# A field-pair interaction tower on one core: sums of eight units, half-height transposes, and a batch cut into five uneven pieces

## What is computed

```python
p = e[:, ROW_IDX]            # first field of each of the 496 pairs
q = e[:, COL_IDX]            # second field
z = jnp.einsum('bne,hne,bnh->bn', p, kernel, q)
h = jnp.concatenate([z, dense_ctx], axis=1)      # 496 + 16 = 512
h = jnp.maximum(h @ W_top1 + b_top1, 0.0)        # 512
h = jnp.maximum(h @ W_top2 + b_top2, 0.0)        # 256
y = h @ W_top3                                   # 1
```

## Time and profile before

| what | us |
|---|---|
| median of 3 runs | 491.37 |
| lowest and highest | 490.74, 492.25 |
| the profiled execution, its own time | 490.84 |
| span of that execution, first to last instruction | 488.7 |
| PE busy | 433.7 |
| DVE busy | 308.0 |
| POOL busy | 242.4 |
| ACT busy | 35.9 |

### The profile page before, as it was taken

How to read it: one execution, slowest core, us unless ns; L and a number is a source line. 1 busy time by engine, 2 the same in 40 slices (tenths; PEclk the granted TensorE clock), 3 DMA queues, 4 the chain that set the end, 5 groups by cost and what they waited for, 6 DMA issues and landing times.

```text
span 488.7 us, 7990 instructions
## 1 busy us (share of the span) xinstructions
PE 433.7 (89%) x3424; PEld 273.8 (56%) x3424; DVE 308.0 (63%) x321; ACT 35.9 (7%) x69; POOL 242.4 (50%) x260
## 2 busy tenths in 40 slices
PE   0227359999999999999999999999999999999986
PEld 0115226665665666666655666666556666666645
DVE  0113418878876646778876547888875557888840
ACT  1000000000001110000001010000001100000002
POOL 5777777777777776651537775462356000000000
PEclk9999859999999999999999999999999999999999
DMA  6677941111111111000101111100001000000000
GB/s 145 155 168 161 213 143 28 29 25 28 28 28 27 26 28 26 24 19 4 24 12 29 26 28 23 20 21 10 15 18 29 0 2 2 2 0 1 1 1 0
DMA packets 13619, 19.18 MB, mean 39 GB/s; under 512 B 5584, under 2 KB 6928, under 8 KB 13584
## 3 DMA queue, kind: packets, MB, share of 16 engines
q1 hardware_dynamic: 5392, 10.27, 8.8%
q0 software_dynamic: 8192, 8.40, 8.2%
HBM read 18.65 MB, written 0.00 MB: 38 GB/s over the span
## 4 chain that ended last, share of the span: by engine, by line
PE 85%; POOL 6%; DMA 3%; issue 2%; SPq 2%; ACT 1%; DVEq 0%; DVE 0%
PE bil L356 47%; PE z_ps L375 24%; POOL gathered L240 6%; PE side_ps L389 4%; PE side_ps L326 4%; PE side_ps L395 2%; DMA inner<-in_dense_rows 2%; PE bil L389 1%; DMA gathered<-in_tbl,ids_sb 1%; SPq L193 1%; PE bil L395 1%; PE side_ps L401 1%; ACT emb L252 0%; DMA ids_sb<-in_ids 0%; DVEq L127 0%
## 5 line engine op out<-in xcount | busy, mean ns | idle before, releaser
L311 DVE TENSOR_TENSOR prod<-bil,emb 128x1024 f32<-128x1024 f32 x224 | 261.4, 1218 | 121.7 <-PE bil L356 121.7
L240 POOL DMA_INDIRECT gathered<-in_tbl,ids_sb x256 | 242.2, 946 | 134.6 <-issue 74.4
L356 PE MATMUL bil<-emb,k_sb 64*128 64x256 f32 x2048 | 250.2, 390 | 3.6 <-ACT emb L252 3.6
L356 PEld LDWEIGHTS bil<-emb,k_sb 64*128 64x128 f32 x2048 | 193.0, 189 | 73.5 <-DVE prod L311 30.7
L375 PE MATMUL z_ps<-prod,sel_sb 128*32 128x512 f32 x960 | 125.9, 604 | 1.6 <-DVE prod L311 1.6
L375 PEld LDWEIGHTS z_ps<-prod,sel_sb 128*32 128x32 f32 x960 | 26.9, 110 | 61.9 <-issue 42.0
L326 PE MATMUL side_ps<-ident_sb,gathered 128*128 128x128 f32 x128 | 22.3, 300 | 31.3 <-DMA gathered<-in_tbl,ids_sb 31.3
L303 DVE TENSOR_TENSOR prod<-bil,emb 128x512 f32<-128x512 f32 x32 | 21.9, 684 | 38.6 <-PE bil L356 29.1
L252 ACT ACTIVATE emb<-side_ps 128x512 f32<-128x512 f32 x32 | 19.2, 599 | 316.6 <-PE side_ps L326 316.6
L375 PE MATMUL z_ps<-inner,sel_sb 128*32 128x512 f32 x64 | 30.2, 619 | 13.7 <-DMA inner<-in_dense_rows 13.7
L326 PEld LDWEIGHTS side_ps<-ident_sb,gathered 128*128 128x128 f32 x128 | 14.3, 148 | 50.0 <-issue 34.0
(11 more groups left out here) (17 smaller groups left out, 22.7 us busy)
## 6 DMA issues: line engine op xcount, KB each, us to landing
k_sb<-in_k_blocks SPq DMA_DIRECT2D x24, 256.0 KB, 5.0
gathered<-in_tbl,ids_sb POOLq DMA_INDIRECT x256, 2.4
k_sb<-in_k_blocks SPq DMA_DIRECT2D x8, 192.0 KB, 5.9
inner<-in_dense_rows SPq DMA_DIRECT2D x64, 1.0 KB
w_sb<-in_w SPq DMA_DIRECT2D x1, 1024.0 KB, 9.2
k_sb<-in_k_blocks SPq DMA_DIRECT2D x8, 64.0 KB, 4.9
w_sb<-in_w SPq DMA_DIRECT2D x1, 512.0 KB, 10.2
ids_sb<-in_ids SPq DMA_DIRECT2D x1, 128.0 KB, 2.1
```

The source lines that it names most:

```text
L240: pool.indirect_dma_start(gathered[:, n % GATHER_RING, t, f * EMBED:(f + 1) * EMBED], None, tables[field], bass.IndirectOffsetOnAxis(ap=id ...
L311: dve.tensor_tensor(out, x_y[:, :, :], both.to_broadcast([P, 2, W]), ALU.mult)\
L356: last = pe.matmul(out[:, s, i * CHUNK:(i + 1) * CHUNK], k_sb[rows, n, :], e[rows, j, :], start=True, stop=True)
```

## The change

Three things change together.

The batch goes through in five pieces, of 128, 128, 256, 256 and 256 samples (`WIDTHS`). All loops over pieces run five times, and in the first two pieces every matmul, product, copy and gather of a quad is half as wide (a quad has four gathers there).

A sum takes eight units instead of four. For that `prod` has twelve places instead of ten and `inner` four instead of two; SP therefore places the dense rows of the first four quads early.

A quad is transposed by pieces of 64 rows: for each tile of 128 samples and each couple, one transpose for the upper 64 samples and one for the lower, with a 64 x 64 part of the identity, into the two banks of a `bil` place. Transposes and units take turns in the ring of three places (`USES`), and each waits for the use three before it: for DVE if that was a unit, for ACT's copy if that was a quad. The copy to `emb` reads both banks of the place and puts the halves in order. `side_ps` is left to the head, whose steps come one unit earlier and no longer wait for the copies of quads.

```diff
-CHUNK = 256
-CHUNKS = BATCH // CHUNK
-SUBS = CHUNK // P
+WIDTHS = [128, 128, 256, 256, 256]
+CHUNKS = len(WIDTHS)
+FROM = [sum(WIDTHS[:q]) for q in range(CHUNKS)]
+CHUNK = max(WIDTHS)
...
-W = 2 * CHUNK
+BANK = 512
...
-BIL_RING, PROD_RING, IN_RING, GATHER_RING = 3, 10, 2, 6
-BATCH_UNITS = 4
+BIL_RING, PROD_RING, IN_RING, GATHER_RING = 3, 12, 4, 6
+BATCH_UNITS = 8
 BATCHES = NUNIT // BATCH_UNITS
-GROUP_BATCHES = 8
+GROUP_BATCHES = 32 // BATCH_UNITS
...
-PIECE_UNITS = [6, 10, 14, 18]
+PIECE_UNITS = [5, 9, 13, 17]
...
+USES = []
+for _u in range(NUNIT):
+    USES += [("quad", n) for n in TRANSPOSED_AT[_u]] + [("unit", _u)]
+BANKS_OF = {use: at % BIL_RING for at, use in enumerate(USES)}
+BEFORE = {use: USES[at - BIL_RING] for at, use in enumerate(USES) if at >= BIL_RING}
...
-        inner = sb("inner", [P, IN_RING, W])
+        inner = sb("inner", [P, IN_RING, 2, CHUNK])
...
-                    for t in range(SUBS):
+                    for t in range(WIDTHS[q] // P):
                         field = 4 * k + f
                         pool.indirect_dma_start(
...
-                act.activation(emb[:, q % 2, 2 * k:2 * k + 2, :].rearrange("p c b -> p (c b)"), side_ps[:, :],
-                               ACT.Copy).then_inc(emb_kept, 1)
+                w = WIDTHS[q]
+                banks = bil[BANKS_OF["quad", n]][:, :, 0:w].rearrange("p s (x b) -> p x s b", b=EMBED)
...
+                act.activation(out, banks, ACT.Copy).then_inc(emb_kept, 1)
...
+                elif w == CHUNK:
+                    both = e[:, c:c + 2, :].rearrange("p c b -> p (c b)").unsqueeze(1)
+                    dve.tensor_tensor(out, x_y[:, :, :], both.to_broadcast([P, 2, BANK]), ALU.mult)\
+                       .then_inc(unit_multiplied, 1)
                 else:
...
+                    both = e[:, c:c + 2, :].unsqueeze(1)
+                    dve.tensor_tensor(out.rearrange("p j (c b) -> p j c b", c=2),
+                                      x_y[:, :, 0:2 * w].rearrange("p j (c b) -> p j c b", c=2),
+                                      both.to_broadcast([P, 2, 2, w]), ALU.mult).then_inc(unit_multiplied, 1)
...
-                if n:
-                    pe.wait_ge(emb_kept, n)
-                pieces = kept_before(u)
-                if pieces:
-                    pe.wait_ge(head_kept, pieces)
+            def wait_banks(use):
+                kind, at = BEFORE.get(use, (None, 0))
+                if kind == "unit":
+                    pe.wait_ge(unit_multiplied, at + 1)
+                elif kind == "quad":
+                    pe.wait_ge(emb_kept, at + 1)
+
+            def transpose_quad(n):
+                pe.wait_ge(quad_gathered[n % GATHER_RING], gathered_count(n))
+                wait_banks(("quad", n))
+                tiles = WIDTHS[n // QUADS] // P
                 for c in range(2):
-                    for t in range(SUBS):
-                        last = pe.transpose(side_ps[:, c * CHUNK + t * P:c * CHUNK + (t + 1) * P],
-                                            gathered[:, n % GATHER_RING, t, c * P:(c + 1) * P], ident_sb[:, :])
+                    for t in range(tiles):
+                        for s in range(2):
+                            rows = slice(s * EMBED, (s + 1) * EMBED)
+                            at = (c * tiles + t) * EMBED
+                            last = pe.transpose(bil[BANKS_OF["quad", n]][:, s, at:at + EMBED],
+                                                gathered[rows, n % GATHER_RING, t, c * P:(c + 1) * P],
+                                                ident_sb[rows, rows])
                 last.then_inc(quad_transposed, 1)
...
-                if u >= BIL_RING:
-                    pe.wait_ge(unit_multiplied, u - BIL_RING + 1)
-                out, e = bil[u % BIL_RING], emb[:, q % 2, :, :]
+                wait_banks(("unit", u))
+                w = WIDTHS[q]
+                out, e = bil[BANKS_OF["unit", u]], emb[:, q % 2, :, 0:w]
...
-                quads = sum(len(TRANSPOSED_AT[v]) for v in range(u + 1))
-                pe.wait_ge(emb_kept, quads)
```

More of the change, by code:

```diff
@@ L153, in interaction_tower @@
         y_sb = sb("y_sb", [P, TILES])
-        bil = [pb(f"bil{i}", [P, 2, W]) for i in range(BIL_RING)]
-        z_ps = pb("z_ps", [P, W])
-        side_ps = pb("side_ps", [P, W])
+        bil = [pb(f"bil{i}", [P, 2, BANK]) for i in range(BIL_RING)]
+        z_ps = pb("z_ps", [P, BANK])
+        side_ps = pb("side_ps", [P, BANK])
         ids_loaded = sem("ids_loaded")
@@ L176, in interaction_tower, with gathered_count @@
         block = ctx.enter_context(nc.Block())
+        def gathered_count(n):
+            return 16 * 4 * sum(WIDTHS[i // QUADS] // P for i in range(n % GATHER_RING, n + 1, GATHER_RING))
         def batch_of(unit):
@@ L290, in _ @@
         def _(dve):
-            dve.memset(inner[:, :, CHUNK:W], 0.0).then_inc(inner_cleared, 1)
+            dve.memset(inner[:, :, 1, :], 0.0).then_inc(inner_cleared, 1)
             for u in range(NUNIT):
                 q, (k, m, c) = u // NU, UNITS[u % NU]
-                x_y, out, e = bil[u % BIL_RING], prod[:, u % PROD_RING, :, :], emb[:, q % 2, :, :]
+                w = WIDTHS[q]
+                x_y, e = bil[BANKS_OF["unit", u]], emb[:, q % 2, :, 0:w]
+                out = prod[:, u % PROD_RING, :, 0:2 * w]
                 dve.wait_ge(unit_done, u + 1)
@@ L302, in _ @@
                         dve.wait_ge(batch_reduced, batch_of(inner_unit(n - IN_RING)) + 1)
[L303 to L305 removed]
+                    dve.tensor_tensor(out[:, 0, :].rearrange("p (j b) -> p j b", j=2), x_y[:, :, 0:w],
+                                      e[:, a:a + 1, :].to_broadcast([P, 2, w]), ALU.mult)
@@ L355, in bilinear @@
                             j = 2 * k + 1 if s == 0 else 2 * k
-                        last = pe.matmul(out[:, s, i * CHUNK:(i + 1) * CHUNK], k_sb[rows, n, :], e[rows, j, :],
+                        last = pe.matmul(out[:, s, i * w:(i + 1) * w], k_sb[rows, n, :], e[rows, j, :],
                                          start=True, stop=True)
@@ L369, in reduce_batch @@
                         col, r = row // 32, row % 32
-                        moving = prod[:, u % PROD_RING, i, :]
+                        moving = prod[:, u % PROD_RING, i, 0:2 * WIDTHS[q]]
                         if m is None and i == 1:
@@ L388, in head @@
                         for g in range(GROUPS):
-                            last = pe.matmul(bank[:, j * CHUNK:(j + 1) * CHUNK], w1_sb[:, g, n * P:(n + 1) * P],
-                                             z_rows(g), start=g == 0, stop=g == GROUPS - 1)
+                            last = pe.matmul(bank[:, j * w:(j + 1) * w], w1_sb[:, g, n * P:(n + 1) * P],
+                                             z_rows(q, g), start=g == 0, stop=g == GROUPS - 1)
                 elif PIECES[i] == "l2":
@@ L394, in head @@
                         for g in range(MT1):
-                            last = pe.matmul(bank[:, n * CHUNK:(n + 1) * CHUNK], w2_sb[:, g, n * P:(n + 1) * P],
-                                             h1_sb[:, g, :], start=g == 0, stop=g == MT1 - 1)
+                            last = pe.matmul(bank[:, n * w:(n + 1) * w], w2_sb[:, g, n * P:(n + 1) * P],
+                                             h1_sb[:, g, 0:w], start=g == 0, stop=g == MT1 - 1)
                 else:
                     pe.wait_ge(head_kept, done + MT1 + MT2)
-                    for t in range(SUBS):
+                    for t in range(w // P):
                         for g in range(MT2):
@@ L417, in _ @@
                 for n in TRANSPOSED_AT[u]:
-                    transpose_quad(u, n)
+                    transpose_quad(n)
                 bilinear(u)
```

47 lines of the change are left out of this document (26 added, 21 removed).

## The result

The changed kernel takes 495.13 us (median; 491.31 for the kernel before beside it), a ratio of 1.0081 with a 95% interval of 1.0066 to 1.0096: slower by 0.8%, as forecast (493, slower). The profiled execution took 493.93 us for a span of 492.1.

What follows compares the result with a forecast made beforehand. It took PE to bound the kernel from 75 us on, after waits for dense features. Start 54.5, then 33.7, 61.3, 101.8, 108.9 and 130.2 gave a 490.4 us span, 493 for the median; range 485.5 to 503.5.

Steps and rivals of the forecast that it cites:

- dense row lands: Start: quad 4's dense row, issued behind k_sb and the head weights, lands at 54.5 us (52.5 to 58).
- piece 1: Second 128-row piece: eight narrow eight-unit batches of 6.54, head 7.1, quads and first copy 1.9; 61.3 us.
- last piece and tail: End of the span: 126.7 before, +5.3 for batches, -3.5 for transposes, +1.7 for a longer last sum; 130.2 us.
- wide batch without a quad: 256-row pieces: eight units and their sum take 11.68 us instead of 11.02, held by DVE through three banks; +0.66.
- narrow batch: 128-row pieces: eight units and their sum take 6.54 us, at a product pitch of 0.62; half of before is 5.51.
- Rival A: Start gains more: dense row near 50.5, before 51.5; median 489 us, or 485 if transposes hide entirely; chance 0.25.
- Rival D: Eight-unit batches are not held by DVE: 10.67 us each, 456 us in all; chance 0.02.
- +5.3 for the batches: 256-row piece: the cost of eight-unit batches, each 0.66 us dearer through DVE's pace.
- -3.5 for the transposes: 256-row piece: 64-row transposes save 0.35 to 0.54 us per quad, 3.5 a piece, with ends of 0 and 4.3.
- the turn in the ring: Transposes sharing the three bil banks wait for DVE, with PE's next units queued behind: up to 0.2 us per quad.
- rival C: Products at 128 rows take 0.69 us apiece, or transposes still cost 0.59: 497 to 503 us; chance 0.20.
- Rival B: Weights bind at 128 columns: a unit stays at 0.86 us, +28, 521 us in all; chance 0.07.

Runs made afterwards that it cites:

- e7: Changed kernel with products of wide units, other than a quad's first, cut to 512 of 1024 elements: 471.58 us in one execution.
- e8: Kernel before with the same cut of wide products to half, as a control: 489.46 us in one execution.
- e1: Changed kernel with sums of four units instead of eight, all else kept: 483.07 us, 0.9835 of the kernel before.
- e6: Kernel before with sums of eight units alone, plus the changed kernel's rings (twelve product places, four dense-row places): 485.25 us, ratio 0.9887.
- e5: Changed kernel with sums of four units, eight places in inner and four wide pieces: 469.20 us, 0.9566 of the kernel before.
- e10: Kernel before with 64-row transposes alone, in the ring of bil, and head steps a unit earlier: 485.50 us, ratio 0.9891.
- e2: Changed kernel with four pieces of 256 rows instead of five uneven ones: 488.25 us, 0.9964 of the kernel before.

## Why the prediction was right, step by step

| step of the sum | predicted, us | measured, us |
|---|---|---|
| dense row lands | 54.5 | 54.30 |
| rest of piece 0 | 33.7 | 34.14 |
| piece 1 | 61.3 | 61.17 |
| piece 2 | 101.8 | 102.17 |
| piece 3 | 108.9 | 109.23 |
| last piece and tail | 130.2 | 131.09 |
| wide batch without a quad | 11.68 | 11.69 |
| narrow batch | 6.54 | 6.41 |
| span | 490.4 | 492.1 |

**The start.** One stall took the place of the other as predicted: the dense row of quad 4 is issued behind all of `k_sb` and the head's weights. Rival A, a landing before 51.5, didn't come about. The SP queue of after shows why (start, duration, line and transfer):

```profile
5.96 29.91 SPq L205 DMA_DIRECT2D k_sb<-in_k_blocks  x38
...
37.10 6.93 SPq L233 DMA_DIRECT2D w_sb<-in_w  x1
44.07 1.29 SPq L234 DMA_DIRECT2D b_sb<-in_b  x1
45.41 1.23 SPq L235 DMA_DIRECT2D b_sb<-in_b  x1
46.68 11.73 SPq L217 DMA_DIRECT2D inner<-in_dense_rows  x10
```

`k_sb` is issued by 35.9 and the two large head weights by 37.1; three tiny transfers then hold SP until 46.68, and the row lands 7.6 us after that. But issued is not landed. For the weight transfers the DMA view of after gives size and us from issue to landing (the one of 512 KB took 17.0), and the windows show the DMA engines until then:

```profile
w_sb<-in_w SPq DMA_DIRECT2D x1, 1024.0 KB, 17.2
...
w_sb<-in_w SPq DMA_DIRECT2D x1, 1.0 KB, 16.8
```

```profile
12.00:48.00 36.00, 24.68 (x296) 20.05 (x294) 17.94 (x36) 2.30 (x6) 27.31 (x29) 1.00 1.05 230
48.00:53.00 5.00, 0.00 (x0) 0.00 (x0) 0.68 (x3) 0.00 (x0) 3.77 (x4) 0.78 1.08 325
```

The engines are full (shares of 1.05 to 1.08), and the weights land together between 53.1 and 53.9, even the one of 1 KB issued at 37.10; the dense row comes 0.4 later. So my way to its time, bytes over GB/s, was the mechanism, at nearly the rates that I took from before (226 and 301). The issues that held SP are a side matter: a row issued in place of that 1 KB would hardly have landed sooner than it did. One reading was loose: of the 67 us that I called waiting, PE is busy for 20.5.

**The eight-unit batch.** DVE's pace with three banks is the cause: e7 takes half of DVE's work away and gets the predicted 10.68, e8 does the same where the sum is of four units and gets nothing, and e1 goes back to four units and gets 12 us. Rival D is out.

**A wide piece: right in sum, wrong in both terms.** The prediction had +5.3 for the batches and -3.5 for the transposes. Four kernels give the middle piece in all four combinations, in us:

| | sums of four | sums of eight |
|---|---|---|
| transposes of 128 rows, own bank | 107.13 (before, e8) | 108.29 (e6) |
| transposes of 64 rows, in the ring, head steps a unit earlier | 105.28 (e1, e5), 105.27 (e10) | 109.23 (after), 109.25 (e2) |

The two parts don't add. Sums of eight cost 1.16 beside the old transposes and 3.95 beside the new; the second row wins 1.85 beside sums of four and loses 0.94 beside sums of eight. Three steps failed. I charged the hold of 0.66 to all eight batches and the 0.59 of a quad to before, but in a batch that PE spends waiting for DVE the old transposes cost 0.03 (11.72 against 11.69), so there was nothing left for the new ones to save. I put the turn in the ring at up to 0.2 a quad: at the start of a run that held (0.25 in all, e10, where I took 0.24), but a quad inside a run of eight takes 0.52 more than none (12.21 against 11.69), near the 0.59 of rival C. And for the head I counted nothing, where its earlier place alone gave 0.8 a piece beside sums of four (e10); what it gives beside sums of eight no run separates.

From sum to sum, after against e6, the first batch of a wide piece wins 0.9 (254.81 to 269.83 against 137.82 to 153.72; its two quads stand behind a sum and a head step), three with a quad inside a run lose 0.5 to 0.6 each, and the others are equal. That 5.3 - 3.5 = 1.8 came near the measured 2.1 was luck: the two errors, some 4 us each when the sums are taken first, have opposite signs. With the old transposes kept, as in e6, a wide piece would have been about 1 us faster: I had no step that could see that.

**Narrow pieces.** Size right (6.41 against 6.54; half of before would be 5.51), and the reason too. The timeline of after in piece 1, the loads of one unit, then a run of eight units and one of three:

```profile
139.50 0.52 PEld L390 LDWEIGHTS bil<-emb,k_sb 64*128 64x128 f32 x8 [0.41 <-issue]
...
139.50 4.42 PEld L390 LDWEIGHTS bil<-emb,k_sb 64*128 64x128 f32 x64 [0.41 <-issue]
139.50 4.61 PE L390 MATMUL bil<-emb,k_sb 64*128 64x128 f32 x64
140.26 4.87 DVE L337 TENSOR_TENSOR prod<-bil,emb 128x512 f32<-128x512 f32 x8 [1.29 <-PE bil L390]
...
145.90 1.42 PEld L390 LDWEIGHTS bil<-emb,k_sb 64*128 64x128 f32 x24 [0.41 <-issue]
145.90 1.61 PE L390 MATMUL bil<-emb,k_sb 64*128 64x128 f32 x24
```

The first three units, which three banks can't hold up, show what a unit costs PE: their loads take 1.42, those of one 0.52, so 0.45 for a further unit (I took 0.47; half of a wide one is 0.43). From the fourth on a unit takes (4.61 - 1.61) / 5 = 0.60, and products come every (4.87 - 0.69) / 7 = 0.60: PE goes at DVE's pace here as well, though it counts as busy for all 6.41 us of such a batch, since matmuls in flight cover the gaps. Five units at 0.15 more are some 0.75 of the 0.90 that a narrow batch loses. e1's narrow batches of four still take 6.31 for eight units: DVE holds only the fourth unit of each, but runs and sums start twice as often, and that doesn't halve with the width (argued from these pitches; no run isolates it). Piece 1's 61.3 hides some luck: eight batches of 6.41 are 51.3 instead of 52.3, the head took 6.5 instead of 7.1, and so quads and the first copy 3.4 instead of 1.9.

Rival B is out (0.45 a unit, not 0.86). The rule of the Trainium skill behind it (TensorE: Matmul & The Clock Gate, "The mechanism"), that loads overlap matmuls only across row groups, isn't borne out at this width either: all loads of a run go to the same two row groups, and they are busy in 4.42 of the 4.61 us in which matmuls are. Rival C's first half is out with the pitch of 0.60.

**The last 2 us.** The last piece and tail took 0.9 more than computed, and the median lies 1.2 above the profiled execution's 493.93, where for before it lay 0.5 above. After's executions spread further (492.02 to 497.12), and with the clock: the mean granted clock is 0.996 in the fastest and 0.985 in the slowest. Why it differs between executions stays open.

## What to carry to other kernels

Before making runs on one engine longer, compare the paces of producer and consumer: a ring hides a slower consumer only for about as many steps as it has places, and past that the run goes at the consumer's pace (1.13 us a unit here, not 0.86). Costs of two edits add only while the same engine binds in both; work that is dear in a stage that its engine bounds is free in a stage where that engine waits, so each edit is to be priced in the order that the other one leaves. An edit run alone may still carry a second one: 0.8 of the 1.86 us that e10's pieces won came from head steps that had moved by one unit. And when a wait is for a small transfer that stands behind a large one in the same queue, give it room to be issued first: one number did that for the kernel before, for 2.8%.

## What the runs showed of the hardware that was not expected

On SP's queue in after, the issue of a head weight transfer of 1 KB (L233) took 6.93 us and the two biases after it 1.29 and 1.23, while the two large weight transfers ahead took 0.60 and 0.50. In before the same three, issued from 56.43 on, took 0.50, 0.43 and 0.43.

The trace doesn't say what held them in after. It put the issue of the dense rows off to 46.68, but their landing by some 0.4 us at most, if they, like the 1 KB, would have had to wait for the large weights. Issuing those three after the dense rows wasn't tried.

The eight half-height transposes of a wide quad take 0.46 us in flight where four of 128 rows took 0.66 (e6), and at the start of a run they delay the next work by 0.30 instead of 0.59. So the 64-row form did win PE time; inside a run it was lost again by where the result was put.
